# Rank weights on 128 partitions, a block-diagonal wkr, one copy of qrT, and new orders, in a gated cross-attention block with an FFN

## The chip, the cores and the metric

One core of a Trainium2 chip runs the whole kernel. The metric is the device time of one execution in microseconds; the median of several runs is quoted. The profile is of one execution.

## The reference

```
x = x + tanh(g_xattn) * attention(layernorm(x), ctx_512)      # x (4, 256, 256), ctx (4, 256, 64)
x = x + tanh(g_ffn)   * ffn(layernorm(x))

attention, 16 heads, K = 128, DCQ = 192, R = 64, D_C = 64:
  q_hk   = hidden_q @ Wq.T                 # per head 128
  q_big  = q_hk @ w_kc_q                   # 128 -> 192
  q_r    = q_big @ W_qr                    # 192 -> 64
  k_r    = rope(kv_c) @ W_kr               # 64 -> 64
  attn   = softmax(q_r @ k_r.T)            # no scale
  out    = ((attn @ rope(kv_c)) @ w_kc_kv) @ Wo.T

ffn: layer_norm; thought = last row @ agg_w + agg_b;
  4 times: thought += gelu(layer_norm(thought) @ d1_w + d1_b) @ d2_w + d2_b
  out = layer_norm(x + sigmoid(x @ gate_w + gate_b) * (thought @ bc_w + bc_b))
```

All is float32.

## The kernel before

The weights on the way from x to the scores are folded first: for each head W_qr and w_kc_q make qrT (64 x 128), qrT and W_kr make qk (128 x 64), and qk with Wq makes a part of A (foldA), so that the scores of a head are (x_norm A) kv^T. In the same way w_kc_kv and Wo make B (foldB). Heads go in four groups of four (NG = 4, HG = 4). Where precision needs it, a float32 operand is split: ScalarE writes a rounded half (A_hi, xT_hi, q_split), VectorE the rest by subtraction (A_lo, xT_lo), and TensorE adds three products (split_product, lines 898 to 902).

x goes in eight units of 128 rows (NU = 8): units 0 to 3 mix rows of all four batches, the last rows of each batch first, units 4 to 7 take one batch each. Steps of a unit or pair of units: x_stats (mean and variance on VectorE; POOL makes rstd, lines 550 to 558), x_norm, xT (transposes), gq (q of a group for two units), smax (scores for the row maxima, VectorE reduces them, line 749), shiftT (the maxima as a row), q_hi_load (a DMA that moves half of q to the other partitions), st (transposed scores, ScalarE's Exp makes probs), pv, ctxT, out and out_rest, y_stats, y_norm, yT, gate, and at the end f_y, f_pre, f_norm and the store. The FFN's thought chain (c_stats, thoughtT, agg, up, down, downT, bc, bc_rows) runs beside it from unit 0's last rows; its weights are cut into three bfloat16 parts by POOL (w_parts, lines 559 to 573: 8 chunks of d1_w, then 8 of d2_w, which is loaded into the same tile w_rest once the first eight are done, lines 483 to 485).

The order of the work on every engine is written out by hand-held tables: SLOTS gives each step a slot on each engine that takes part, make_plan sorts them, and each engine goes through its list in order, waiting on semaphores. SP issues the loads, all in one queue. PSUM is four rings of two banks: qk and smax; qrT and st; foldB and pv; all others. A step on TensorE waits until its bank is free (claim).

The steps that are changed: load_wqr and load_wkcqT, two DMAs for each group, on 96 partitions (the 192 of DCQ as 96 x 2), load_wkrT on 64 partitions; qrT on TensorE (lines 928 to 939), 8 products per group with 96 rows; the two halves of its result in PSUM, for odd and even heads, are copied to the same 64 partitions of qrT, the odd one by ScalarE (line 607), then the even one by VectorE (line 725), which waits for ScalarE; qk (lines 940 to 952), 8 products per group with 64 rows and 64 columns. WARM is five products on cleared data at the start (line 906), keep five at the end (line 1067).

Of the kernel before, what the change touches and what calls it, by code (L numbers as in the profile page):

```python
# [33 lines left out]
HG = 4  # L34
NG = H // HG
JQ = DCQ // 2
# [31 lines left out]
        "ctxT": (61, 67, 107, 108, 127, 137, 170, 178, 204, 214, 238, 239, 258, 264, 268, 270),  # L68
        "out": (77, 121, 143, 187, 234, 245, 267, 271),
        "out_rest": (79, 122, 145, 188, 235, 246, 269, 272),  # L70
        "yT": (116, 153, 198, 231, 251, 257, 273, 275),
        "gate": (132, 161, 230, 243, 254, 262, 274, 277),
        "thoughtT": (98, 111, 135, 158, 190, 211),
        "agg": (101,),
        "up": (117, 138, 173, 194),
        "down": (123, 146, 181, 201),
        "downT": (126, 149, 186, 205),
        "bc": (216,),
        "bc_rows": (221, 224, 228),
# [2 lines left out]
    "dve": {
        "kvT": (0, 7),
        "qrT": (3, 5, 8, 9),
        "foldA": (11, 14, 22, 24),
        "foldB": (32, 35, 45, 46),
        "x_stats": (1, 2, 12, 13, 15, 16, 21, 23),
        "x_norm": (4, 6, 17, 18, 39, 52, 70, 71),
        "xT": (10, 31, 69, 130),
        "gq": (19, 20, 28, 30, 38, 44, 51, 55, 79, 81, 88, 89, 141, 148, 150, 171),  # L90
        "smax": (25, 26, 27, 29, 33, 34, 36, 37, 40, 41, 42, 43, 47, 48, 49, 50, 57, 58, 60, 61, 63, 64, 66, 67, 68,
# [14 lines left out]
        "down": (110, 131, 157, 172),
        "downT": (113, 135, 159, 176),
# [1 line left out]
        "f_y": (80, 127, 204, 205, 222, 224, 240, 244),
        "f_pre": (195, 196, 212, 213, 225, 228, 242, 245),  # L110
        "f_norm": (202, 203, 217, 218, 235, 236, 246, 247),
    },
    "act": {
        "g_tanh": (30,),
        "kvT": (0, 3),
        "qrT": (1, 2, 7, 8),
        "qk": (4, 5, 11, 14),
        "foldA": (9, 10, 15, 16),
        "foldB": (20, 21, 24, 25),
        "xT": (6, 19, 46, 74),  # L120
        "gq": (12, 13, 17, 18, 22, 26, 32, 33, 47, 49, 53, 54, 81, 85, 86, 100),
        "shiftT": (23, 36, 51, 59, 71, 92, 109, 126),
# [1090 lines left out]
```

## Time and profile before

| | |
|---|---|
| time, median of 3 runs | 212.63 us (212.58 to 213.01) |
| the profiled execution | 213.38 us |
| its span, first to last instruction | 211.4 us |
| busy in the span | TensorE 193.6, VectorE 169.2, ScalarE 96.6, POOL 71.9 us |
| mean granted TensorE clock | 0.949 |

The span leaves out 2.0 us of the execution that lie around the instructions. PE is TensorE, DVE VectorE, ACT ScalarE, SPq the queue of SyncE that issues the DMAs. A matmul instruction's duration includes the filling of the array, so the durations of single ones overlap; a merged row gives the time from the first start to the last end. One float32 product is two instructions in these rows. Times are in us from the start of the span.

### The profile page before, as it was taken

The page shows a single profiled execution, that of the slowest core. Times are in us where ns is not written, and L with a number is a line of the kernel's source. Part 1 is how long each engine was busy: PE and PEld are TensorE (multiplying, and loading weights), DVE is VectorE, ACT ScalarE, POOL GpSimd, SP SyncE. Part 2 cuts the span into 40 slices and gives each one's busy share as a digit, 9 for nine tenths or more (in the row PEclk, how much of TensorE's full clock was granted, in tenths as well). Part 3 has the DMA queues.
Part 4 walks back from the last instruction along what each step waited for, and adds up shares of the span by engine and source line. Part 5 has one row for each costly group of instructions (what it writes and reads, how often), then busy time and mean ns, then how long its engine had stood idle before and what let it go on. Part 6 is the DMA issues. An engine that isn't in the chain of part 4 may idle for free.

```text
span 211.4 us, 6214 instructions
## 1 busy us (share of the span) xinstructions
PE 193.6 (92%) x2533; PEld 169.7 (80%) x2533; DVE 169.2 (80%) x399; ACT 96.6 (46%) x177; POOL 71.9 (34%) x151
## 2 busy tenths in 40 slices
PE   7289979999999999999999999999999999998860
PEld 5078969679889997889999998999887888887730
DVE  4742699999799999996995999395973787899975
ACT  2215354443954355555193567548325243471120
...
GB/s 172 229 250 337 416 416 238 102 5 99 3 199 105 0 5 102 51 3 3 33 72 3 28 75 5 3 0 3 5 172 31 2 3 51 0 44 13 25 25 50
DMA packets 10499, 17.85 MB, mean 84 GB/s; under 512 B 1052, under 2 KB 6436, under 8 KB 9960
## 3 DMA queue, kind: packets, MB, share of 16 engines
...
## 4 chain that ended last, share of the span: by engine, by line
PE 57%; DVE 20%; POOL 8%; DMA 5%; issue 5%; ACT 2%; SPq 1%; POOLq 0%; DVEq 0%; ACTq 0%
PE ps L1032 9%; PE ps L1019 7%; PE ps L1000 6%; PE ps L1021 6%; PE ps L900 4%; DMA wqr<-in_wqr 4%; PE ps L901 4%; PE ps L902 4%; PE ps L936 4%; DVE row_max L749 3%; DVE bn L675 2%; PE ps L1121 2%; PE ps L1110 2%; PE ps L1081 2%; PE ps L1042 2%
## 5 line engine op out<-in xcount | busy, mean ns | idle before, releaser
L638 ACT ACTIVATE probs<-ps 128x512 f32<-128x512 f32 x64 | 36.2, 596 | 33.8 <-PE ps L1021 32.9
L749 DVE TENSOR_REDUCE row_max<-ps 128x2 f32<-128x512 f32 x64 | 41.7, 681 | 5.6 <-PE ps L1000 5.1
L556 POOL TENSOR_SCALAR var_eps<-mean_var 128x1 f32<-128x1 f32 (+1 forms) x29 | 7.3, 251 | 114.0 <-DVE mean_var L676 113.4
L1032 PEld LDWEIGHTS ps<-kv,probs 128*64 128x64 f32 x1024 | 31.2, 137 | 3.0 <-issue 2.0
L1032 PE MATMUL ps<-kv,probs 128*64 128x65 f32 x1024 | 33.6, 223 | 0.0
L1019 PE MATMUL ps<-q_hi,kv_lo 128*128 128x512 f32 x64 | 28.3, 443 | 0.2 <-DMA q_hi<-shift 0.2
L1021 PE MATMUL ps<-q_split,kv_hi 128*128 128x512 f32 x64 | 25.5, 398 | 0.0
L1000 PE MATMUL ps<-kv_hi,q_split 128*128 128x256 f32 x128 | 24.9, 300 | 0.4 <-DVE q_split L743 0.4
L1000 PEld LDWEIGHTS ps<-kv_hi,q_split 128*128 128x128 f32 x128 | 19.1, 189 | 3.9 <-issue 1.9
L900 PE MATMUL ps<-xT_lo,A_hi 128*128 128x256 f32 x64 | 18.9, 295 | 0.1
L900 PE MATMUL ps<-B_lo,ctxT_hi 128*128 128x256 f32 x64 | 18.5, 289 | 0.0
L901 PE MATMUL ps<-xT_hi,A_hi 128*128 128x256 f32 x64 | 18.1, 282 | 0.0
L902 PE MATMUL ps<-xT_hi,A_lo 128*128 128x256 f32 x64 | 18.0, 282 | 0.0
L901 PE MATMUL ps<-B_hi,ctxT_hi 128*128 128x256 f32 x64 | 18.0, 282 | 0.0
L902 PE MATMUL ps<-B_hi,ctxT_lo 128*128 128x256 f32 x64 | 18.0, 282 | 0.0
L557 POOL TENSOR_TENSOR rstd<-var_eps,minus_half 128x1 f32<-128x1 f32 (+1 forms) x29 | 17.1, 590 | 2.4
L624 ACT ACTIVATE q_split<-ps 64x512 fp32r<-64x512 f32 x16 | 9.4, 590 | 16.7 <-PE ps L902 16.7
L641 ACT ACTIVATE ctxT_hi<-ps 128x512 fp32r<-128x512 f32 x16 | 9.4, 597 | 13.2 <-PE ps L1042 13.2
L762 DVE TENSOR_TENSOR ctxn<-ps,prob_sum_inv 128x256 f32<-128x256 f32 x32 | 13.6, 424 | 1.1
L1019 PEld LDWEIGHTS ps<-q_hi,kv_lo 128*128 128x128 f32 x64 | 12.3, 193 | 2.3 <-issue 0.7
L1021 PEld LDWEIGHTS ps<-q_split,kv_hi 128*128 128x128 f32 x64 | 12.4, 194 | 1.0
L900 PEld LDWEIGHTS ps<-xT_lo,A_hi 128*128 128x128 f32 x64 | 12.1, 190 | 0.9 <-DVE q_split L743 0.3
(133 smaller groups left out, 405.7 us busy)
## 6 DMA issues: line engine op xcount, KB each, us to landing
...
wq<-in_wq SPq DMA_DIRECT2D x4, 512.0 KB, 12.5
...
w_rest<-in_d_w SPq DMA_DIRECT2D x2, 1024.0 KB, 12.8
...
wqr<-in_wqr SPq DMA_DIRECT2D x4, 192.0 KB, 10.1
x<-in_x SPq DMA_DIRECT2D x2, 256.0 KB, 10.3
```

The costliest lines, as they stand in the source:

```text
L557: pool.tensor_tensor(rstd[0:rows, n:n + 1], var_eps[0:rows, n:n + 1], minus_half[0:rows, :], ALU.pow).then_inc(rstd_made, 1)
L624: act.activation(q_part(U, j, 0, lower), q_from(e, lower), ACT.Copy)
L638: act.activation(probs[:, n % PROBS_BUFS, lb, :], bank(e), ACT.Exp).then_inc(free[place[e]], 1)
L749: dve.reduce_max(row_max[:, s % 2, 2 * j:2 * j + 2], bank(e).rearrange("p (h l) -> p h l", h=2), AX.X).then_inc(free[place[e]], 1)
L762: dve.tensor_tensor(dst, r[:, :, 0:DC], prob_sum_inv[:, :].unsqueeze(2).to_broadcast([P, HG, DC]), ALU.mult).then_inc(free[place[e]], 1)
L900: pe.matmul(dst, a_hi, b_lo, start=first, stop=False)
L901: pe.matmul(dst, a_hi, b_hi, start=False, stop=False)
L902: return pe.matmul(dst, a_lo, b_hi, start=False, stop=last)
L1000: ins = pe.matmul(bank(e)[:, i * S:(i + 1) * S], q_split[s // 2 % 2][:, c:c + P], kv_hi2[:, kv_batch(s, j // 2), :], start=True, stop=True)
L1019: pe.matmul(bank(e), kv_lo[:, b, ls], q_hi[:, u % 2, g * HG * P:(g + 1) * HG * P], start=True, stop=False)
L1021: pe.matmul(bank(e), kv_hi2[:, b, ls], q_split[U % 2][:, q], start=False, stop=True).then_inc(done, 1)
L1032: ins = pe.matmul(bank(e)[q:q + 64, hh * (DC + 1):(hh + 1) * (DC + 1)], probs[:, n % PROBS_BUFS, lb, hh * P + q:hh * P + q + 64], kv1[:, k ...
```

## The change

The rank weights of a pair of heads are laid out in one tensor of 128 partitions and 640 columns: the first 128 of the 192 rows of w_kc_q (transposed) for the even head, then, for both heads, the last 64 rows, the even head's on partitions 0 to 63 and the odd head's on 64 to 127, then the first 128 of the odd head, then the four pieces of W_qr to match, with zeros where the other head's rows stand. One DMA loads the two pairs of a group (load_rank, 640 KB). qrT is again 8 products per group, now over 128 rows. Its result keeps odd heads on the upper 64 partitions, and ScalarE alone copies it, 128 x 256. wkr is block-diagonal over a pair of heads (128 x 128, 512 KB in all), so qk is 4 products per group over 128 rows and 128 columns.

All orders are new. On TensorE qrT 0 goes ahead of kvT 0, foldA 0 and 1 ahead of qk 2, qrT 3 behind gq 0,1, and keep behind the last gate. On VectorE x_stats 0 and 1 come first, and x_stats 2 to 6 ahead of gq 0,0. On POOL out 0 (it scales two rows by the tanh) goes ahead of x_stats 3, and all 16 w_parts ahead of y_stats 0. On SP the order is consts, ctx, rank 0, rank 1, x 0, wkr, rank 2, wq 0, wq 1, x 1, the rest of x, rows, rank 3, wq 2, wq 3, w1, wkckv, wo 0, wo 1, q_hi 0, gate and agg, q_hi 1, shiftT 0, w2, shiftT 1; before it was ctx, consts, wkcqT 0, wkrT, wkcqT 1, wqr 0, x 0, wqr 1, wkcqT 2 and 3, wqr 2 and 3, wq 0, wq 1, x 1, the rest of x, wq 2, wq 3, wkckv, wo 0, w1, wo 1, gate and agg, rows, q_hi 0, vecs, shiftT 0, q_hi 1, shiftT 1, w2.

```diff
-JQ = DCQ // 2
+RANK = 3 * P + 4 * R
...
-        "kvT": (0, 3),
-        "qrT": (1, 2, 7, 8),
+        "kvT": (1, 3),
+        "qrT": (0, 2, 7, 13),
-        "foldA": (9, 11, 15, 16),
+        "foldA": (8, 9, 15, 16),
...
-        "keep": (276,),
+        "keep": (277,),
...
-        "kvT": (0, 7),
-        "qrT": (3, 5, 8, 9),
-        "foldA": (11, 14, 22, 24),
...
+        "kvT": (2, 5),
+        "foldA": (7, 9, 19, 22),
+        "x_stats": (0, 1, 8, 10, 11, 12, 13, 18),
+        "x_norm": (3, 4, 16, 17, 36, 37, 57, 60),
+        "y_norm": (78, 111, 136, 165, 190, 210, 231, 235),
...
-        "x_stats": (1, 2, 3, 4, 5, 6, 7, 8),
-        "out": (24, 24, 24, 24, 24, 24, 24, 24),
-        "y_stats": (20, 30, 31, 36, 39, 40, 47, 50),
-        "w_parts": (9, 10, 11, 12, 13, 14, 15, 16, 17, 18, 19, 21, 22, 25, 26, 27),
-        "c_stats": (23, 28, 29, 34, 35),
-        "f_y": (32, 33, 41, 43, 48, 49, 51, 52),
-        "f_pre": (37, 38, 42, 44, 45, 46, 53, 54),
+        "x_stats": (1, 2, 3, 5, 6, 7, 8, 9),
+        "out": (4, 4, 4, 4, 4, 4, 4, 4),
+        "y_stats": (26, 30, 33, 36, 37, 44, 49, 50),
+        "w_parts": (10, 11, 12, 13, 14, 15, 16, 17, 18, 19, 20, 21, 22, 23, 24, 25),
...
-        "load_wkcqT": (2, 4, 8, 9),
-        "load_wqr": (5, 7, 10, 11),
-        "load_wkrT": (3,),
...
-        "load_w1": (20,),
-        "load_w2": (29,),
...
+        "load_rank": (2, 3, 6, 12),
+        "load_wkr": (5,),
...
+        "load_w1": (15,),
...
+        "load_w2": (23,),
...
-        wkrT = sb("wkrT", [R, H * DC], F32, stage)
-        wqr = sb("wqr", [JQ, H, 2, R], F32, stage)
-        wkcqT = sb("wkcqT", [JQ, H, 2, P], F32, stage)
-        qrT = sb("qrT", [R, 2, HG * P], F32, stage)
+        wkr = sb("wkr", [P, H // 2, 2 * DC], F32, stage)
+        rank = sb("rank", [P, H // 2, RANK], F32, stage)
+        qrT = sb("qrT", [P, 2, HG // 2 * P], F32, stage)
...
+                if name == "load_rank":
+                    ps2 = slice(HG // 2 * e[1], HG // 2 * (e[1] + 1))
+                    sp.dma_start(rank[:, ps2, :], t["rank"][:, ps2, :]).then_inc(rank_in[e[1]], 16)
...
-                    act.activation(qrT_cols(e[1], 1), bank(e)[upper, 0:HG // 2 * P].rearrange("p (i k) -> p i k", k=P),
-                                   ACT.Copy).then_inc(qrT_odd_copied, 1)
+                    act.activation(qrT[:, e[1] % 2, :], bank(e)[:, 0:HG // 2 * P], ACT.Copy
+                                   ).then_inc(free[place[e]], 1)
...
-                if name == "qrT":
-                    dve.wait_ge(qrT_odd_copied, e[1] + 1)
-                    filled(dve, e)
-                    dve.tensor_copy(qrT_cols(e[1], 0), bank(e)[lower, 0:HG // 2 * P].rearrange("p (i k) -> p i k", k=P)
-                                    ).then_inc(free[place[e]], 1)
...
-                    pe.wait_ge(wqr_in[g], 16)
-                    pe.wait_ge(wkcqT_in[g], 16)
-                    for hh in range(0, HG, 2):
-                        for j in range(2):
+                    pe.wait_ge(rank_in[g], 16)
+                    for i in range(HG // 2):
+                        w = rank[:, HG // 2 * g + i, :]
+                        for part in range(2):
                             for odd in range(2):
-                                ins = pe.matmul(bank(e)[64 * odd:64 * odd + 64, hh // 2 * P:(hh // 2 + 1) * P],
-                                                wqr[:, HG * g + hh + odd, j, :], wkcqT[:, HG * g + hh + odd, j, :],
-                                                start=(j == 0), stop=(j == 1))
+                                keys = w[:, P:2 * P] if part else w[:, 2 * P * odd:2 * P * odd + P]
+                                queries = w[:, 3 * P + R * (2 * part + odd):3 * P + R * (2 * part + odd + 1)]
+                                ins = pe.matmul(bank(e)[64 * odd:64 * odd + 64, i * P:(i + 1) * P], queries, keys,
+                                                start=(part == 0), stop=(part == 1))
                     ins.then_inc(done, 1)
                 if name == "qk":
 
                     g = e[1]
                     taken(pe, ("qrT", g))
                     if g == 0:
-                        pe.wait_ge(wkrT_in, 16)
-                    for hh in range(HG):
-                        h = HG * g + hh
+                        pe.wait_ge(wkr_in, 16)
+                    for i in range(HG // 2):
                         for k in (0, 64):
-                            ins = pe.matmul(bank(e)[k:k + 64, hh * DC:(hh + 1) * DC],
-                                            qrT[:, g % 2, hh * P + k:hh * P + k + 64],
-                                            wkrT[:, h * DC:(h + 1) * DC], start=True, stop=True)
+                            ins = pe.matmul(bank(e)[k:k + 64, 2 * i * DC:2 * (i + 1) * DC],
+                                            qrT[:, g % 2, i * P + k:i * P + k + 64],
+                                            wkr[:, HG // 2 * g + i, :], start=True, stop=True)
...
+    keys = a["L0_xattn_w_kc_q"].transpose(0, 2, 1)
+    queries = a["L0_xattn_W_qr"]
+    rank = np.zeros((H // 2, P, RANK), np.float32)
+    wkr = np.zeros((P, H // 2, 2 * DC), np.float32)
+    for odd in range(2):
+        rows = slice(64 * odd, 64 * odd + 64)
+        wkr[rows, :, DC * odd:DC * (odd + 1)] = a["L0_xattn_W_kr"][odd::2].transpose(2, 0, 1)
+        rank[:, :, 2 * P * odd:2 * P * odd + P] = keys[odd::2, 0:P]
+        rank[:, rows, P:2 * P] = keys[odd::2, P:DCQ]
+        rank[:, :, 3 * P + R * odd:3 * P + R * (odd + 1)] = queries[odd::2, 0:P]
+        rank[:, rows, 3 * P + R * (2 + odd):3 * P + R * (3 + odd)] = queries[odd::2, P:DCQ]
```

## Rows read from the trace of the kernel before

**Rows 1.** Windows, four stretches: us, busy us (instructions) of each engine, clock, DMA

```profile
core 0: us, PE busy (x) PEld busy (x) DVE busy (x) ACT busy (x) POOL busy (x), PEclk, DMA share, GB/s
4.00:18.00 14.00, 9.27 (x78) 7.21 (x78) 8.21 (x12) 3.50 (x7) 6.03 (x12) 0.68 1.02 240
18.00:34.00 16.00, 14.78 (x230) 13.59 (x231) 10.71 (x26) 7.15 (x14) 4.21 (x12) 0.85 1.02 409
23.40:45.60 22.20, 20.48 (x255) 16.82 (x249) 21.07 (x42) 10.60 (x20) 14.69 (x32) 1.00 0.64 238
45.60:200.50 154.90, 152.36 (x2124) 136.12 (x2124) 130.21 (x325) 78.35 (x143) 45.07 (x89) 0.99 0.16 39
```

**Rows 2.** Chain of waits, in order of time: start us, us, what

```profile
3.34 7.86 DMA wqr<-in_wqr
```

**Rows 3.** Timeline of SP's queue: start us, us, issue

```profile
1.17 0.42 SPq L444 DMA_DIRECT2D consts<-in_consts  x1
...
12.64 0.43 SPq L477 DMA_DIRECT2D w_rest<-in_d_w  x1
```

**Rows 4.** DMA issues of 1.1 to 1.6 us: size, us to landing

```profile
consts<-in_consts SPq DMA_DIRECT2D x1, 192.0 KB, 2.7
```

**Rows 5.** The two loads of w_rest, at 12.64 and 58.4 us

```profile
DMA to landing us min/median/max: 6.3/12.8/19.4
```

**Rows 6.** Windows at two changes of the TensorE clock

```profile
9.00:9.25 0.25, 0.00 (x0) 0.00 (x0) 0.23 (x1) 0.00 (x0) 0.00 (x0) 0.51 0.94 205
22.50:23.00 0.50, 0.50 (x18) 0.50 (x16) 0.00 (x0) 0.30 (x1) 0.00 (x0) 0.84 1.09 418
```

**Rows 7.** Timeline of PE: start us, us, instructions

```profile
11.25 3.80 PE L936 MATMUL ps<-wkcqT,wqr 96*64 96x128 f32 x32 [4.18 <-DMA wqr<-in_wqr]
...
16.02 1.97 PE L949 MATMUL ps<-wkrT,qrT 64*64 64x64 f32 x32
...
24.18 1.15 PE L962 MATMUL ps<-qk,wq 128*64 128x64 f32 x32
...
28.52 0.68 PE L949 MATMUL ps<-wkrT,qrT 64*64 64x64 f32 x16
...
37.85 0.66 PE L925 MATMUL ps<-consts,xn 128*128 128x128 f32 x4
```

**Rows 8.** Groups by shape, first 50 us: busy us, mean ns, idle before

```profile
L675 DVE BATCH_NORM_STATS2 bn<-x 128x6 f32<-128x256 f32 x8 | 3.4, 424 | 2.9 <-DMA x<-in_x 2.8
...
L725 DVE COPY qrT<-ps 64x256 f32<-64x256 f32 x4 | 1.7, 413 | 5.5 <-ACT qrT L607 5.5
L611 ACT ACTIVATE qk<-ps 128x256 f32<-128x256 f32 x4 | 1.5, 382 | 0.4 <-PE ps L949 0.3
L607 ACT ACTIVATE qrT<-ps 64x256 f32<-64x256 f32 x4 | 1.5, 380 | 9.1 <-PE ps L936 9.1
L676 DVE BATCH_NORM_AGGREGATE mean_var<-bn 128x2 f32<-128x6 f32 x8 | 1.5, 182 | 0.3
```

**Rows 9.** Timeline of DVE

```profile
5.51 3.47 DVE L698 MEMSET q_hi<- 64x4096 f32 x1 [0.80 <-issue]
...
24.32 0.69 DVE L730 TENSOR_TENSOR A_lo<-ps,A_hi 128x512 fp32r<-128x512 f32 x1 [0.20 <-ACT A_hi L615]
...
44.86 0.69 DVE L743 TENSOR_TENSOR q_split<-ps,q_split 64x512 fp32r<-64x512 f32 x1
...
73.03 0.40 DVE L682 TENSOR_SCALAR y<-x,mean_var,rstd 128x256 f32<-128x256 f32 x1
```

**Rows 10.** Timeline of POOL

```profile
34.37 0.41 POOL L569 CAST d_parts<-w_rest 128x256 bf16<-128x256 f32 x1
...
52.30 0.67 POOL L572 TENSOR_TENSOR d_parts<-w_rest,d_parts 128x256 bf16<-128x256 f32 x1
64.74 0.40 POOL L569 CAST d_parts<-w_rest 128x256 bf16<-128x256 f32 x1 [11.77 <-DMA w_rest<-in_d_w]
...
72.29 0.57 POOL L557 TENSOR_TENSOR rstd<-var_eps,minus_half 128x1 f32<-128x1 f32 x1
```

More of the change, by code:

```diff
@@ L62 @@
-        "shiftT": (35, 55, 90, 104, 131, 176, 210, 242),
[5 rows of a table removed]
[L68 to L79, printed above, removed]
-        "keep": (276,),
+        "foldA": (8, 9, 15, 16),
+        "foldB": (23, 25, 32, 35),
+        "xT": (6, 24, 44, 139),
+        "gq": (11, 12, 19, 22, 28, 31, 37, 41, 86, 89, 96, 97, 160, 161, 170, 195),
+        "smax": (17, 18, 20, 21, 26, 27, 29, 30, 33, 36, 38, 42, 43, 47, 48, 52, 54, 57, 59, 62, 63, 67, 70, 71, 75,
+            77, 80, 82, 83, 85, 87, 88, 94, 95, 98, 99, 107, 112, 114, 120, 121, 124, 126, 130, 136, 148, 152, 153, 165,
+            166, 171, 173, 179, 187, 202, 204, 208, 214, 215, 219, 222, 224, 226, 229),
@@ new lines @@
+        "shiftT": (34, 56, 76, 105, 127, 169, 209, 240),
[5 rows of a table added]
+        "ctxT": (66, 72, 115, 116, 142, 149, 180, 181, 205, 213, 233, 236, 261, 262, 268, 270),
+        "out": (81, 122, 154, 190, 221, 242, 267, 271),
+        "out_rest": (84, 123, 155, 191, 223, 244, 269, 272),
+        "yT": (108, 132, 201, 232, 248, 252, 273, 275),
+        "gate": (131, 175, 207, 247, 251, 258, 274, 276),
+        "thoughtT": (103, 119, 145, 164, 193, 216),
+        "agg": (110,),
+        "up": (128, 151, 178, 196),
@@ L81 @@
+        "down": (135, 156, 186, 203),
+        "downT": (138, 159, 189, 212),
+        "bc": (220,),
+        "bc_rows": (225, 227, 228),
+        "keep": (277,),
     },
     "dve": {
-        "kvT": (0, 7),
-        "qrT": (3, 5, 8, 9),
-        "foldA": (11, 14, 22, 24),
[L86 to L90, printed above, removed]
@@ L106 @@
[L106 to L107 removed]
+        "up": (112, 130, 151, 167),
+        "down": (116, 133, 156, 170),
+        "downT": (119, 137, 157, 178),
         "bc": (185,),
[L109 to L111 removed]
+        "f_y": (79, 114, 199, 202, 207, 219, 237, 240),
+        "f_pre": (194, 195, 200, 211, 216, 223, 238, 241),
@@ L112 @@
+        "f_norm": (196, 201, 206, 213, 218, 226, 242, 243),
     },
     "act": {
[L114 to L122, printed above, removed]
[3 rows of a table removed]
-        "ctxT": (40, 43, 61, 62, 70, 72, 89, 93, 108, 110, 123, 125, 135, 143, 144, 145),
@@ L127 @@
-        "yT": (63, 79, 103, 119, 132, 136, 146, 147),
-        "gate": (82, 105, 130, 131, 137, 142, 148, 149),
-        "up": (66, 73, 91, 101),
-        "bc_rows": (115, 116, 118),
+        "g_tanh": (11,),
+        "kvT": (1, 3),
+        "qrT": (0, 2, 7, 14),
+        "qk": (4, 5, 10, 15),
+        "foldA": (8, 9, 16, 17),
+        "foldB": (21, 22, 26, 27),
+        "xT": (6, 20, 31, 74),
+        "gq": (12, 13, 18, 19, 23, 24, 28, 34, 51, 52, 55, 56, 85, 86, 90, 103),
+        "shiftT": (25, 37, 48, 59, 67, 88, 109, 125),
[3 rows of a table added]
@@ L131 @@
+        "ctxT": (42, 45, 65, 66, 77, 80, 95, 96, 107, 113, 120, 123, 141, 143, 144, 145),
+        "yT": (61, 69, 105, 119, 130, 134, 146, 147),
+        "gate": (72, 94, 111, 131, 135, 139, 148, 149),
+        "up": (68, 81, 97, 104),
+        "bc_rows": (114, 115, 116),
     },
@@ L193, in steps @@
     return {
-        "load_consts": [()], "load_wkcqT": [(g,) for g in groups], "load_wqr": [(g,) for g in groups],
-        "load_wkrT": [()], "load_wq": [(g,) for g in groups], "load_x": [(U,) for U in halves], "load_x_rest": [()],
+        "load_consts": [()], "load_rank": [(g,) for g in groups],
+        "load_wkr": [()], "load_wq": [(g,) for g in groups], "load_x": [(U,) for U in halves], "load_x_rest": [()],
         "load_ctx": [()], "load_wo": [(i,) for i in halves], "load_wkckv": [()], "load_rows": [()], "load_w1": [()], "load_w2": [()], "load_bc_w": [()],
@@ L428, in ctx_from @@
             return bank(e).rearrange("p (b g q) -> p b g q", b=2, g=H // 2)
-        def qrT_cols(g, odd):
-            return qrT[:, g % 2, :].rearrange("p (i two k) -> p i two k", two=2, k=P)[:, :, odd, :]
         lower, upper = slice(0, 64), slice(64, 128)
@@ L1179, in laid_out @@
         "ctx": a["ctx_512"].reshape(NB, LB, P, DC).transpose(2, 0, 1, 3),
-        "wkrT": a["L0_xattn_W_kr"].transpose(2, 0, 1).reshape(R, H * DC),
-        "wqr": a["L0_xattn_W_qr"].reshape(H, JQ, 2, R).transpose(1, 0, 2, 3),
-        "wkcqT": a["L0_xattn_w_kc_q"].reshape(H, K, JQ, 2).transpose(2, 0, 3, 1),
+        "wkr": wkr,
+        "rank": rank.transpose(1, 0, 2),
         "wq": a["L0_xattn_Wq"].reshape(H, K, D).transpose(1, 0, 2),
```

82 lines of the change are left out of this document (36 added, 46 removed), and 24 rows, old and new, of the table SLOTS.

## The prediction

> **What bounds the kernel now.** I read the windows by stage first, then the chain of waits, then the timelines of SP, PE, DVE and POOL, and the groups by shape. The windows show three regimes. From 45.6 us to 200.5 us TensorE is busy 152.4 of 154.9 us [rows 1], so whatever brings that stage forward brings the end forward, unless something else becomes late. From 23.4 to 45.6 us VectorE is busy 21.1 of 22.2 us [rows 1]: it subtracts rounded halves, takes row maxima and x's statistics, and TensorE waits for it. Before that both wait for loads: the chain starts with the DMA of wqr, 7.86 us from its issue [rows 2], and TensorE, idle for 4.18 us, begins qrT 0 at 11.25 [rows 7].
>
> The loads explain why. With the 16 DMA engines busy all the time (share 1.02), 240 GB/s move from 4 to 18 us and 409 GB/s from 18 to 34 [rows 1]. The break is where the last rank load is through; those of before stand on 96 or 64 partitions, those after on 128. Beside it the clock: TensorE falls to 1.2 GHz (granted 0.51) at 9.0 us, in its idle stretch, and is back at 2.4 GHz only within 22.5 to 23.0 [rows 6], having worked without a break from 11.25.
>
> **The loads after.** 192 + 256 KB of consts and ctx end at 1.17 + 2.7 = 3.9 us [rows 3, 4], and still do: the two change places. Four rank loads of 640 KB and wkr of 512 KB follow instead of 2304 + 256 KB, that is 512 KB more, and four issues fewer. All rows are now 128 partitions by 4 to 5 KB (the nearest: wq, w_rest, in the 409 GB/s stretch), so I take 409 GB/s. 640 KB then take 1.60 us, 512 KB 1.28. Landings: rank 0 at 5.5, rank 1 at 7.1, x 0 at 7.7, wkr at 9.0, rank 2 at 10.6, wq 0 at 11.9, wq 1 at 13.2, x 1 at 13.8, the rest of x at 15.1, the rows at 16.1, rank 3 at 17.7, wq 2 at 19.0, wq 3 at 20.2, w1 at 22.8 (before: 12.64 + 19.4 = 32.0 [rows 3, 5]). The other bound is that 240 GB/s last to 18 us whatever the layout; then wq 0 lands at 3.9 + 3.28 MB / 240 GB/s = 17.6.
>
> The Trainium skill (SBUF — State Buffer, "Door 1: The DMA port swizzle") has a mechanism for the slow stretch: partitions 0 to 63 sit behind eight of the sixteen ports, so 96 partitions load the crowded ports as 128 would. By its 435 GB/s, the early rank loads, x 0 and wkrT (30 KB per partition) would take an estimated 9.0 us; the trace gives them some 14, so the ports alone don't account for it. A figure of the skill speaks against the change's rate: DMA: Bandwidth & Descriptors, "Specifications", limits one core's HBM share to about 358 GB/s. By that w1 would land at 25.5 (estimate), 2.7 us later; the trace disagrees, 409 GB/s over 16 us [rows 1].
>
> **The front of TensorE and VectorE.** qrT passes the same columns as before, with 128 rows instead of 96: 3.80 us for two groups at 1.2 GHz [rows 7], 1.9 a group, and an estimated 0.95 at 2.4 GHz. qk passes the same columns in half as many instructions; a group takes 0.68 us at full clock [rows 7], I take no gain (bounds 0 and half of it, 0.34), since VectorE hides it. The copy of qrT by ScalarE covers 128x256 instead of 64x256: 382 against 380 ns [rows 8], so nothing; ScalarE is idle before it. VectorE loses four copies, 1.7 us, which stood in a stretch where it waited 5.5 us for them [rows 8]; that too is worth nothing by itself, and the 0.41 us it takes from each hand-over is covered by kvT and xT.
>
> At full clock TensorE ends WARM at 5.9, then qrT 0, kvT 0, qrT 1, kvT 1 (0.95 and about 0.6 each) at 9.0, as wkr lands, and qk 0 and 1 at 10.4. VectorE's clearing of q_hi ends at 9.0 [rows 9]. Behind it: two x_stats (0.61 plus a gap, 0.67 each [rows 8]) to 10.3, kvT 0 to 11.0, two x_norm to 11.9. xT's transposes take 0.66 [rows 7], to 12.5; qrT 2 to 13.5; foldA 0 takes 1.15 [rows 7], to 14.6; ScalarE's half 0.6; so VectorE begins A_lo 0 at 15.3 instead of 24.32 [rows 9]. From there to the end of gq 1,0 (45.55 [rows 9]) VectorE's list holds the same operations in another order, and every load they need (wq 3 at 20.2) is in before its turn. So the stretch keeps its 21.2 us, and the front moves by 9.0.
>
> **What takes part of it back.** y_norm 0 waits for a rstd from POOL. In the new order all sixteen w_parts stand ahead of it; before, only eleven did. POOL begins them at the later of w1 (22.8) and x_stats 7, for which VectorE has from 15.3: eight-fold work of A_lo, x_stats, gq and x_norm, 0.69 x 2 + 6 x 0.67 + 2 x 1.4 + 2 x 0.43 = 9.1 us, plus 0.8 of POOL: 25.2. From there eight chunks 18.6 us (34.37 to 52.97), the load of w2 6.3 from its issue (it now stands ahead of shiftT 1 on SP, and goes out at once; before, POOL waited 11.77 us), eight more chunks 18.5, and rstd 0.9 [rows 5, 10]: 44.4 in all, so 69.6. VectorE's new list has three maxima and gq 2,0 more ahead of y_norm 0, five reads of 128x512 at 0.69 [rows 9], 3.4 us: it would be wanted at 73.0 + 3.4 - 9.0 = 67.4. VectorE stands 2.2 us, in order, and the smax banks behind it fill, so TensorE stands too. Net 9.0 - 2.2 = 6.8 us.
>
> Other moves. out 0 on POOL, ahead of x_stats 3, waits for the rows (16.1) and tanh, and takes some 2 us; x_norm 3 needs the result at about 24, so gq 0,0 and 0,1 on VectorE cover it. SP stands at load_w2 until about 43.8; behind it is shiftT 1, wanted at about 50. q_hi 0 follows wo 1, which by the same rate is in at 29.2, about when gq 0,3 ends. keep goes behind the last gate: five products of 512 columns, by foldA's row (2048 in 1.15 us) an estimated 1.4 us no longer in front of it; VectorE is still at unit 6 then, so I take 0 and keep 0 to 1.1 as a gain. The rest of the new order has the same work in a stage where TensorE is full; I take 0 and allow 0.5 either way.
>
> **The sum.** The profiled execution took 213.38 us (span 211.4 and 2.0 around it), 0.75 above the median of the runs. 213.38 - 6.8 = 206.6 on its own scale, 212.63 - 6.8 = 205.8 for the median. A change under 0.2% (0.4 us) could not be told from none.
>
> **Rivals.** (a) The clock falls anyway. TensorE now has work in most of 6 to 10.4 us, where before it had little between WARM and 11.25, but it still waits there for loads and for VectorE; and at half clock it ran from 11.25 to past 22.5 us before it got the full clock back [rows 6, 7]. Worked out: 5.9, two qrT 3.8, two kvT 2.1, two qk 2.0, xT 1.3, qrT 2 1.9, foldA 0 2.3, ScalarE 0.6: A_lo 0 at 19.9, 4.6 us worse. Gain 2.2, time 210.4. The skill (TensorE: Matmul & The Clock Gate, "Part 1") agrees that low recent activity brings the low level.
> (b) The layout does not do what it says: 240 GB/s belong to the start of the kernel, not to 96 partitions. Then wq 0 at 17.6, A_lo 0 at 19.3, gain 2.8, time 209.8. For it: no 128-partition load ran by itself before 18 us, so nothing shows 409 GB/s that early. Against: the break lies where the layout changes.
> (c) TensorE works through y_norm's stall from its queue (gq 2,1, st, pv stand behind): gain 9.0, with keep and the orders up to 10, time 203.6 down to 202.5.
> (d) Slower: y_norm 0 stuck behind POOL. If the slow rate lasts through w1 (7.75 MB at 240 GB/s), w1 lands at 36.2, y_norm 0 comes at 80.6 instead of 73.0 + 3.4 = 76.4: 4.2 slower, 216.8. It decides from a w1 later than 32.0. Against it: 409 GB/s in the stretch of the very same loads.
> (e) Nothing is left because a later wait (the chain of the thoughts, whose agg, up and down now stand later in TensorE's list) holds the end: 212.6.
>
> **Numbers.** Forecast 0.52, (a) 0.20, (b) 0.09, (c) 0.11, (d) 0.04, (e) 0.04. Range 202.5 to 210.5: from (c) to (a) and (b). Faster 0.92, same 0.03, slower 0.05 (part of (e) falls on either side).
>
> **What would show it.** qrT 0 beginning near 6 us; above 350 GB/s from 4 us on; granted clock 1.00 through 9 to 15 us; A_lo 0 near 15; POOL's first chunk near 25 instead of 34.4; y_norm 0 near 69.6 with VectorE waiting for POOL. Wrong would be made by half clock past 12 us, by loads that land a third later, or by a wait behind 80 us that the trace of before does not have.

## The result and the profile after

The changed kernel takes 205.62 us (median of 4 runs, 204.75 to 206.37) against 212.61 us (4 runs, 212.18 to 213.01) beside it: ratio 0.967, 95% interval 0.9625 to 0.9716. The forecast was 205.8 us in a range of 202.5 to 210.5. The profiled execution took 205.26 us, with a span of 203.4. Here and below, ratios and intervals compare undisturbed runs alone, while a median also takes in runs that the chip slowed by some per cent, so a ratio can be nearer to 1 than that of the two medians.

First the windows by stage, which answer to [rows 1]; columns as there.

```profile
core 0: us, PE busy (x) PEld busy (x) DVE busy (x) ACT busy (x) POOL busy (x), PEclk, DMA share, GB/s
4.00:9.00 5.00, 3.07 (x22) 1.98 (x21) 4.19 (x2) 0.00 (x0) 4.46 (x8) 1.00 0.93 277
9.00:18.00 9.00, 8.61 (x134) 7.18 (x132) 4.42 (x10) 5.61 (x12) 1.67 (x4) 0.81 1.03 404
4.00:18.00 14.00, 11.67 (x153) 9.16 (x152) 8.61 (x12) 5.61 (x12) 6.13 (x12) 0.88 0.99 358
9.00:9.50 0.50, 0.50 (x6) 0.47 (x4) 0.00 (x0) 0.38 (x1) 0.00 (x0) 0.71 1.05 311
12.50:13.00 0.50, 0.50 (x8) 0.29 (x8) 0.50 (x2) 0.18 (x1) 0.42 (x3) 0.88 0.99 410
```

The stretch that moved 240 GB/s before moves 358 now, but not evenly: 277 GB/s to 9 us, 404 after it. TensorE's clock falls at 9 us as before, to 1.2 GHz, and is back within 12.5 to 13.0; before it stayed low until past 22.5 [rows 6].

The chain of waits starts with another load than before [rows 2] (first and later pieces: start us, us, what):

```profile
2.58 8.36 DMA x<-in_x
...
10.96 0.44 DVE bn L663
...
12.93 0.69 POOL rstd L545
...
14.20 0.63 PE ps L908 x4
14.83 1.02 PE ps L921 x16
15.86 0.95 PE ps L945 x32
...
16.83 0.61 ACT A_hi L603
```

It is now x 0, landing at 10.94 us, then its statistics, its transposes, qrT 2 and foldA 0 that lead to A_lo 0. TensorE's timeline (start us, us, instructions) shows that the first rank products (7.93 and 9.80) are done before x's transposes are wanted and are no longer the link:

```profile
7.93 1.09 PE L921 MATMUL ps<-rank 128*64 128x128 f32 x16 [1.93 <-DMA rank<-in_rank]
...
9.80 1.97 PE L921 MATMUL ps<-rank 128*64 128x128 f32 x16
...
12.71 1.09 PE L932 MATMUL ps<-wkr,qrT 128*64 128x128 f32 x16
14.20 0.63 PE L908 MATMUL ps<-consts,xn 128*128 128x128 f32 x4 [0.39 <-DVE xn L670]
```

VectorE and POOL, for [rows 9] and [rows 10]:

```profile
10.96 0.43 DVE L663 BATCH_NORM_STATS2 bn<-x 128x6 f32<-128x256 f32 x1 [1.97 <-DMA x<-in_x]
17.46 0.69 DVE L713 TENSOR_TENSOR A_lo<-ps,A_hi 128x512 fp32r<-128x512 f32 x1 [1.27 <-ACT A_hi L603]
...
38.20 0.69 DVE L726 TENSOR_TENSOR q_split<-ps,q_split 64x512 fp32r<-64x512 f32 x1
...
70.52 0.41 DVE L670 TENSOR_SCALAR y<-x,mean_var,rstd 128x256 f32<-128x256 f32 x1
```

```profile
27.02 0.40 POOL L557 CAST d_parts<-w_rest 128x256 bf16<-128x256 f32 x1
...
50.48 0.40 POOL L557 CAST d_parts<-w_rest 128x256 bf16<-128x256 f32 x1 [4.85 <-DMA w_rest<-in_d_w]
...
69.41 0.57 POOL L545 TENSOR_TENSOR rstd<-var_eps,minus_half 128x1 f32<-128x1 f32 x1
```

A_lo 0 starts at 17.46 us instead of 24.32: 6.9 earlier. The end of gq 1,0 comes at 38.89 instead of 45.55: 6.7 earlier, so VectorE's stretch kept its length (21.4 us). y_norm 0 starts at 70.52 with no wait in front of it; POOL's rstd is done at 69.98. y_norm 0 stands 2.5 us before its old place with 3.4 us more work ahead of it, 5.9 in all. From y_norm 0 to the end, 132.9 us against 138.4: 5.5 less, of which 3.4 is the work that now lies ahead; the other 2.1 us is taken up below.

### The profile page after: what moved, and what is told of

It reads as the page before. It is cut to its first block, busy times and chain, and to the rows that moved or that the text cites. A ratio compares the mean times of both kernels' runs of the same rounds, so it can differ in the third digit from the quotient of the medians.

```text
span 203.4 us, 6138 instructions
## 1 busy us (share of the span) xinstructions
PE 188.3 (93%) x2501; PEld 164.3 (81%) x2501; DVE 167.3 (82%) x395; ACT 96.2 (47%) x177; POOL 73.4 (36%) x151
## 4 chain that ended last, share of the span: by engine, by line
PE 62%; DVE 22%; DMA 6%; issue 5%; POOL 2%; ACT 1%; SPq 1%; POOLq 0%; DVEq 0%
PE ps L1015 11%; PE ps L983 7%; PE ps L883 7%; PE ps L885 6%; PE ps L884 6%; PE ps L1002 5%; PE ps L1004 4%; DMA x<-in_x 4%; DVE row_max L732 4%; DVE bn L663 3%; PE ps L1104 2%; PE ps L1025 2%; PE ps L1093 2%; PE ps L1064 2%; DVE fin_in L862 2%
## 5 line engine op out<-in xcount | busy, mean ns | idle before, releaser
L1002 PE MATMUL ps<-q_hi,kv_lo 128*128 128x512 f32 x64 | 27.7, 432 | 0.3 <-DMA q_hi<-shift 0.3
L983 PE MATMUL ps<-kv_hi,q_split 128*128 128x256 f32 x128 | 25.5, 300 | 0.3 <-DVE row_max L732 0.2
L1004 PE MATMUL ps<-q_split,kv_hi 128*128 128x512 f32 x64 | 25.2, 394 | 0.0
L545 POOL TENSOR_TENSOR rstd<-var_eps,minus_half 128x1 f32<-128x1 f32 (+1 forms) x29 | 18.1, 624 | 2.4
L883 PEld LDWEIGHTS ps<-xT_lo,A_hi 128*128 128x128 f32 x64 | 12.2, 190 | 1.3 <-DVE A_lo L713 0.8
```

What stands on the lines that cost most here:

```text
L545: pool.tensor_tensor(rstd[0:rows, n:n + 1], var_eps[0:rows, n:n + 1], minus_half[0:rows, :], ALU.pow).then_inc(rstd_made, 1)
L883: pe.matmul(dst, a_hi, b_lo, start=first, stop=False)
L983: ins = pe.matmul(bank(e)[:, i * S:(i + 1) * S], q_split[s // 2 % 2][:, c:c + P], kv_hi2[:, kv_batch(s, j // 2), :], start=True, stop=True)
L1002: pe.matmul(bank(e), kv_lo[:, b, ls], q_hi[:, u % 2, g * HG * P:(g + 1) * HG * P], start=True, stop=False)
L1004: pe.matmul(bank(e), kv_hi2[:, b, ls], q_split[U % 2][:, q], start=False, stop=True).then_inc(done, 1)
```

## The experiments

The twelve kernels ran in three groups on chips that did not repeat alike: the kernel before gave medians of 213.31 (212.02 to 217.15), 212.79 (208.18 to 216.89) and 212.25 us (208.75 to 216.67) beside them. So ratios are compared within a group, and places in the traces carry the finer readings. Those too vary by themselves: in its three profiles the changed kernel starts A_lo 0 at 17.46, 16.86 (after_again) and 17.89 us (after_third).

**layout_only: the new layout under the old orders.** The changed kernel with all the orders of before.

```diff
-        "load_rank": (2, 3, 6, 12),
-        "load_wkr": (5,),
+        "load_rank": (2, 4, 8, 10),
+        "load_wkr": (3,),
...
-        "kvT": (1, 3),
-        "qrT": (0, 2, 7, 13),
+        "kvT": (0, 3),
+        "qrT": (1, 2, 7, 8),
```

> The changed layout (rank weights on 128 partitions, wkr block-diagonal, one copy by ScalarE) with the orders of the kernel before. Theory 1, the loads are the lever and the layout brings their rate: the last rank load is through near 14 us instead of 18, VectorE begins A_lo 0 near 19.5 to 20.5 instead of 24.3, the kernel takes 207.5 to 209. Theory 2, the orders bring the gain: 211.5 to 212.6. The stage behind 45 us is unchanged in order, so a gain in the front that is lost behind it would show as A_lo 0 early and a time near 212.

**orders_only: the new orders with the old layout.** The three rank loads take the places of rank and wkr; both halves of qrT's copy are back.

```diff
-        "load_wkcqT": (2, 4, 8, 9),
-        "load_wqr": (5, 7, 10, 11),
-        "load_wkrT": (3,),
+        "load_wkcqT": (2, 3, 6, 12),
+        "load_wqr": (2.5, 3.5, 6.5, 12.5),
+        "load_wkrT": (5,),
```

> The layout of the kernel before (96 and 64 partitions, two loads for each group, two copies of qrT) with the new orders. Theory 1: the loads still run at about 240 GB/s until the rank weights of three groups are in; wq 0 now stands behind three groups instead of four, 576 KB less, so A_lo 0 comes some 2.5 us earlier than 24.3 and the kernel takes 209 to 210.5. Theory 2: 206 to 207.

**padded: only the partitions changed.** The kernel before, its rank weights and wkr filled up with zeros to 128 partitions: 1 MB more to load, the products still read 96 and 64 of them.

```diff
-        wqr = sb("wqr", [JQ, H, 2, R], F32, stage)
-        wkcqT = sb("wkcqT", [JQ, H, 2, P], F32, stage)
+        wqr = sb("wqr", [P, H, 2, R], F32, stage)
+        wkcqT = sb("wkcqT", [P, H, 2, P], F32, stage)
...
-        "wqr": a["L0_xattn_W_qr"].reshape(H, JQ, 2, R).transpose(1, 0, 2, 3),
+        "wqr": padded(a["L0_xattn_W_qr"].reshape(H, JQ, 2, R).transpose(1, 0, 2, 3)),
```

> The kernel before with wkcqT, wqr and wkrT padded with zeros to 128 partitions; a third more bytes for the first two and twice for the last, the products read the same 96 and 64 partitions, all orders as before. If the rate of a load hangs on how many partitions it covers: from 9 us on above 390 GB/s, the last rank load through near 15 us instead of 18.2 although 1 MB more is moved, and 210 to 211.5. If the low rate belongs to the number of bytes or to the first 18 us of the kernel: the rate stays near 240, the last rank load comes at 20 us or later, and the kernel takes 214 or more.

Windows of the three kernels in that order (two of layout_only, three of orders_only, two of padded):

```profile
4.00:9.00 5.00, 2.70 (x17) 1.94 (x18) 4.19 (x2) 1.18 (x2) 4.46 (x8) 0.88 0.94 332
9.00:18.00 9.00, 7.43 (x78) 5.99 (x76) 3.96 (x9) 3.45 (x8) 1.58 (x4) 0.69 1.00 375
```

```profile
9.00:18.00 9.00, 6.66 (x85) 5.78 (x86) 4.55 (x11) 4.48 (x9) 1.61 (x4) 0.76 1.03 297
18.00:29.00 11.00, 8.23 (x128) 7.75 (x126) 8.68 (x21) 4.43 (x10) 5.76 (x12) 0.81 1.03 359
29.00:34.00 5.00, 5.00 (x77) 4.76 (x74) 1.34 (x4) 1.58 (x3) 4.01 (x9) 0.50 0.91 372
```

```profile
4.00:9.00 5.00, 2.69 (x9) 1.48 (x8) 4.19 (x2) 1.18 (x2) 4.45 (x8) 1.00 0.89 300
9.00:18.00 9.00, 5.20 (x40) 4.14 (x42) 3.37 (x9) 0.92 (x3) 1.59 (x4) 0.55 1.02 375
```

layout_only: 208.08 us, ratio 0.9788 (0.9739 to 0.9837), A_lo 0 at 20.19 us. orders_only: 211.20, ratio 0.9948 (0.9905 to 0.9991), A_lo 0 at 19.97. padded: 214.48, ratio 1.0061 (1.0025 to 1.0097), A_lo 0 at 25.61. Three readings:

The rate follows the partitions that the loads cover. padded moves 300 and then 375 GB/s, 348 over the 14 us in which the kernel before moved 240 [rows 1]; the number of loads and the length of a row on a partition are as before, so neither of these was the brake. It is slower all the same, where 210 to 211.5 us were expected: more bytes go first (x 0 is in at 13.92 us instead of 12.49), and the clock is low for most of the stretch from 9 us (0.55), so a rate is not yet an early landing. The layout of the change gets the rate without the padding.

By ratio and 212.6 us, the layout alone gives 4.5 us and the orders alone some 1.1. The changed kernel did not run in this group: it gave 7.0 in its own, and clear_by_act below, which differs from it only in who clears q_hi, gave 5.9 here. So the layout is two thirds to three quarters of the gain, and 0.3 to 1.4 us would be what the two give only together; the intervals, about 1 us to either side each, don't settle that.

The orders alone bring A_lo 0 forward by 4.35 us, more than the 2.5 expected, and lose it again. TensorE, working without a break from 29 to 34 us, does so at 1.2 GHz, and VectorE is busy for 1.3 of these 5 us. Ahead of it stands this wait (PE timeline):

```profile
28.27 1.12 PE L949 MATMUL ps<-wkrT,qrT 64*64 64x64 f32 x16 [2.77 <-DVE qrT L725]
```

VectorE's half of the copy of qrT 3 stands behind the first two gq in its list, and TensorE waits for it. This asks what the copy by ScalarE alone is worth:

**split_copy: the changed kernel with two half copies again.**

```diff
-                    act.activation(qrT[:, e[1] % 2, :], bank(e)[:, 0:HG // 2 * P], ACT.Copy
-                                   ).then_inc(free[place[e]], 1)
+                    act.activation(qrT[upper, e[1] % 2, :], bank(e)[upper, 0:HG // 2 * P], ACT.Copy
+                                   ).then_inc(qrT_odd_copied, 1)
...
+                if name == "qrT":
+                    dve.wait_ge(qrT_odd_copied, e[1] + 1)
+                    filled(dve, e)
+                    dve.tensor_copy(qrT[lower, e[1] % 2, :], bank(e)[lower, 0:HG // 2 * P]).then_inc(free[place[e]], 1)
```

> The changed kernel with qrT copied out in two halves as before, the upper 64 partitions by ScalarE, then the lower 64 by VectorE (first in its list, between kvT 0 and x_norm 0, behind xT 0, behind gq 0,1). Theory: each copy costs VectorE 0.41 us; the two of the first groups stand ahead of x_stats and x_norm, where VectorE waits for x 0 anyway, the last stands in the full stretch. 0.3 to 0.8 us slower than the changed kernel. If the copy by ScalarE alone is worth nothing: within 0.2 us.

207.82 us, ratio 0.9819 (0.9767 to 0.9872); the changed kernel beside it (after_again) 206.64, ratio 0.9791 (0.9737 to 0.9845). The intervals overlap, so the times don't show a loss; the traces do. A_lo 2 waits, and y_norm 0 comes at 73.07 us instead of 69.48. Of these 3.6 us, 1.0 is a front that was later already (A_lo 0 at 17.90 against 16.86), within what the changed kernel does by itself; 2.5 arise behind it, not the 0.3 to 0.8 expected. PE, then DVE timeline of split_copy:

```profile
25.81 1.12 PE L938 MATMUL ps<-wkr,qrT 128*64 128x128 f32 x8 [3.00 <-DVE qrT L715]
```

```profile
29.30 0.69 DVE L719 TENSOR_TENSOR A_lo<-ps,A_hi 128x512 fp32r<-128x512 f32 x1 [2.32 <-ACT A_hi L605]
```

The copy costs VectorE 0.42 us, and TensorE 3.0 us of waiting, by its place behind four subtractions and no longer by its length. The place (after the first two gq) was mine; a better one may cost less, and was not tried.

**clear_by_act: does the clearing of q_hi slow the loads?** VectorE's memset of 64x4096 replaced by four ScalarE instructions that write zeros.

```diff
-            dve.memset(q_hi[64:P, :, :].bitcast(F32), 0.0).then_inc(q_hi_cleared, 1)
...
+            for i in range(4):
+                ins = act.activation(q_hi[64:P, i // 2, S * NB * (i % 2):S * NB * (i % 2 + 1)],
+                                     kv_lo[64:P, :, :].rearrange("p b l -> p (b l)").bitcast(F32), ACT.Copy, scale=0.0)
```

> The changed kernel, but the 3.5 us clearing of q_hi is done by ScalarE (four copies scaled by zero, from about 4.7 to 9 us) instead of VectorE. In the changed kernel the loads run at 277 GB/s from 4 to 9 us and at 412 from then on, and VectorE's clearing ends at 9.0. If that clearing slows the loads: the rate from 5.5 to 9 us rises to about 400, rank 0 and x 0 land 1 to 2 us earlier, and the kernel takes 204 to 205. If the low rate belongs to the start of the kernel: the rate is 270 to 290 from 4 to 9 us again, x 0 lands at 11.0 again, and the time is that of the changed kernel within 0.5 us (VectorE waits for x 0 anyway; ScalarE is ready for qrT 0 only just in time).

206.28 us, ratio 0.9723 (0.964 to 0.9806): as the changed kernel. 286 GB/s from 4 to 9 us, A_lo 0 at 17.86 us. So it does not matter which engine clears. ScalarE's clearing falls in the same 5 us, and a kernel without any was not tried; but padded and front_loads move 379 and 425 GB/s from 8 to 9 us while VectorE clears, so the clearing need not slow a load.

**after_again** is the changed kernel once more, beside split_copy and the next two.

> The changed kernel once more, as the measure for the three kernels beside it. Expected as before: about 0.967 of the kernel before.

206.64 us, ratio 0.9791 (0.9737 to 0.9845), 4.4 us by ratio where the first group had 7.0, and the intervals don't meet: the gain is some 2 to 3 per cent, and its size differs between chips. y_norm 0 at 69.48 us, here with a wait of 0.24 for POOL: its rstd and VectorE arrive together.

**y_early: y_stats 0 on POOL behind the eleventh chunk, as before.**

```diff
-        "y_stats": (26, 30, 33, 36, 37, 44, 49, 50),
+        "y_stats": (20.5, 30, 33, 36, 37, 44, 49, 50),
```

> The changed kernel with y_stats 0 on POOL behind the eleventh w_parts chunk, as in the kernel before, instead of behind the sixteenth. In the trace of the changed kernel POOL has the rstd of y_stats 0 at 69.98 us and VectorE, busy until 70.5, begins y_norm 0 at 70.52, so it does not wait. Theory 1 (no price of w_parts at this front): the time stays within 0.4 us of the changed kernel's, up (w_parts 1 ends 0.9 us later for down 0) or down. Rival (the forecast's 2.2 us stall is there, only hidden in the profile): 1 us or more faster.

213.08 us, ratio 1.0142 (1.009 to 1.0194): 6.4 us slower than after_again, the whole gain gone. Neither theory said so. POOL's and then VectorE's timeline:

```profile
69.88 0.22 POOL L544 TENSOR_SCALAR var_eps<-mean_var 128x1 f32<-128x1 f32 x1 [10.47 <-DVE mean_var L664]
...
83.45 0.56 POOL L545 TENSOR_TENSOR rstd<-var_eps,minus_half 4x1 f32<-4x1 f32 x1
```

```profile
84.05 0.40 DVE L670 TENSOR_SCALAR thought_norm<-last_rows,mean_var,rstd 4x256 f32<-4x256 f32 x1 [5.94 <-POOL rstd L545]
```

With w2 in early, POOL reaches y_stats 0 at 59.4 us, ten before VectorE has its input; it stands, in order, and the last five chunks and the rstd of the thoughts behind them come late, the latter at 83.45 us where after_third has it at 75.76. (1.5 of these 7.7 us is a later front, A_lo 0 at 19.36 against 17.89; the other 6.2 agree with the 6.4 of the medians.) TensorE, busy 3.05 of the 5 us from 78 to 83, falls to 1.2 GHz behind it. So all chunks ahead of y_stats 0, which the forecast booked as a cost, is what the early w2 wants.

**w1_late: w1 loaded behind wo 1.**

```diff
-        "load_w1": (15,),
+        "load_w1": (18.5,),
```

> The changed kernel with the load of w1 behind wo 1 in SP's queue, so that it lands near 31 us instead of 25.9 and POOL begins w_parts 4 us later. If the in-order wait of VectorE at y_norm 0 passes on one for one: y_norm 0 comes near 74, 3.5 us later than 70.5, and the kernel takes 3 to 3.5 us more than the changed one. If TensorE works through the wait from its queue and VectorE catches up: at most 1 us more.

212.52 us, ratio 1.0022 (0.9979 to 1.0064): 5.9 us slower than after_again. VectorE's timeline:

```profile
75.87 0.41 DVE L670 TENSOR_SCALAR y<-x,mean_var,rstd 128x256 f32<-128x256 f32 x1 [4.71 <-POOL rstd L545]
```

w1 lands at 32.7 us, later than the 31 expected. Against the first profile of the change, whose front ends at the same time (A_lo 0 at 17.46 and 17.47), POOL's rstd is 5.9 us late, y_norm 0 5.4, of which VectorE stands 4.71, and the span is 6.1 longer (209.5 against 203.4). The stall at y_norm 0 passes on in full: TensorE has no queue that hides it, which is against rival (c), and rival (d)'s mechanism is real, only its condition did not hold. The expected 3 to 3.5 us had left out that POOL was just in time already.

The last four ran together: **after_third**, the changed kernel; **warm8**, with more warming; **front_loads** and **front_and_pool**, an attempt at a faster front.

> The changed kernel once more, on the chip of the three runs beside it. Both theories: 205 to 207 us, ratio near 0.968 to 0.98 as before.

```diff
-WARM = 5
+WARM = 8
```

> The changed kernel with 8 instead of 5 matmuls that warm TensorE at the start. Theory: the front is a chain through loads and VectorE (the x 0 load lands at 10.96 us, A_lo 0 at 17.46), so a clock that stays up between 9 and 12 us can shorten only qrT 1 and the two qk, which end before xT 0 is wanted; A_lo 0 stays within 0.3 us of 17.46, the time within 0.5 us of the control. Rival (the half clock from 9.2 to 12.6 us is on the path): A_lo 0 comes 1 us or more earlier and the time falls by about 1 us.

after_third 206.08 us, ratio 0.9781 (0.9649 to 0.9914); warm8 205.70, ratio 0.979 (0.9671 to 0.9909). after_third's PE and DVE timelines, then warm8's:

```profile
10.54 1.98 PE L921 MATMUL ps<-rank 128*64 128x128 f32 x16
```

```profile
17.89 0.69 DVE L713 TENSOR_TENSOR A_lo<-ps,A_hi 128x512 fp32r<-128x512 f32 x1 [1.21 <-ACT A_hi L603]
```

```profile
9.57 1.09 PE L921 MATMUL ps<-rank 128*64 128x128 f32 x16
10.60 0.65 PE L900 MATMUL ps<-consts,kv 128*65 128x128 f32 x4
12.67 1.09 PE L932 MATMUL ps<-wkr,qrT 128*64 128x128 f32 x16 [1.42 <-DMA wkr<-in_wkr]
14.54 0.63 PE L908 MATMUL ps<-consts,xn 128*128 128x128 f32 x4 [0.77 <-DVE xn L670]
```

```profile
17.80 0.69 DVE L713 TENSOR_TENSOR A_lo<-ps,A_hi 128x512 fp32r<-128x512 f32 x1 [1.27 <-ACT A_hi L603]
```

In one, qrT 0 and qrT 1 take twice as long as in the other; A_lo 0 starts 0.09 us apart, far less than the changed kernel varies by itself. What warm8 saves, TensorE waits for wkr (1.42 us) and for x's norm (0.77). The clock does not set the front now; the loads do.

**front_loads: x 0 and wkr ahead of rank 1, wq 0 and 1 ahead of rank 2**, and foldA 0 and 1 ahead of qrT 2.

```diff
-        "load_rank": (2, 3, 6, 12),
-        "load_wkr": (5,),
-        "load_wq": (7, 8, 13, 14),
-        "load_x": (4, 9),
+        "load_rank": (2, 5, 8, 12),
+        "load_wkr": (4,),
+        "load_wq": (6, 7, 13, 14),
+        "load_x": (3, 9),
...
-        "foldA": (8, 9, 15, 16),
+        "foldA": (6.3, 6.6, 15, 16),
```

> The changed kernel with x 0 and wkr loaded ahead of rank 1, wq 0 and wq 1 ahead of rank 2, and foldA 0 and 1 ahead of qrT 2 on TensorE and ScalarE. Theory (the late load of x 0 is what the front lost against the forecast): x 0 lands at about 9 us instead of 10.96, A_lo 0 starts at 15 to 16 us instead of 17.46. VectorE then reaches y_norm 0 about 1.5 us earlier, but POOL's chain (first chunk at 27.02, rstd of y_stats 0 at 69.4) moves by less than that, since its first chunk waits for w1, which lands at 25.9; so the net is a gain of 0.3 to 1 us and VectorE waits about 1 us for POOL before y_norm 0. Rival (the loads at the start are slow whatever comes first): whichever load is second or third is slow, x 0 stays near 10.5 us and A_lo 0 near 17; time as the control.

**front_and_pool: front_loads, and w1 ahead of wq 2, the last x_stats ahead of x_norm 2.**

```diff
-        "x_stats": (0, 1, 8, 10, 11, 12, 13, 18),
+        "x_stats": (0, 1, 8, 10, 11, 12, 13, 15.5),
...
-        "load_w1": (15,),
+        "load_w1": (12.5,),
```

> The kernel front_loads with w1 loaded ahead of wq 2 and the last x_stats ahead of the third x_norm on VectorE, so that POOL may begin its chunks near 25 us instead of 27. Theory (the front and POOL's chain are both at the edge, so both must move for a gain): first chunk at 24.5 to 25.5 us, rstd of y_stats 0 at 67 to 68.5, no wait at y_norm 0, 1.2 to 2 us faster than the control. Rival: wq 2 and wq 3 come late by w1's 2.5 us, foldA 2 waits for them and TensorE or VectorE loses what the rest gained: time as the control or slower.

208.71 us, ratio 0.9899 (0.9739 to 1.006), and 207.43 us, ratio 0.9885 (0.9748 to 1.0023): neither is faster than after_third beside them (2.6 and 1.4 us slower by the medians), and the intervals don't tell them from it. front_loads, DVE and then PE:

```profile
9.02 0.43 DVE L663 BATCH_NORM_STATS2 bn<-x 128x6 f32<-128x256 f32 x1
...
17.05 0.69 DVE L713 TENSOR_TENSOR A_lo<-ps,A_hi 128x512 fp32r<-128x512 f32 x1 [0.70 <-ACT A_hi L603]
```

```profile
11.54 1.09 PE L921 MATMUL ps<-rank 128*64 128x128 f32 x16 [1.60 <-DMA rank<-in_rank]
```

x 0 is in before VectorE asks for it, 1.9 us earlier than in the change, and A_lo 0 gains 0.4 us (0.8 against after_third), no more than the changed kernel varies: now rank 1 is late, 11.5 us. The first group needs consts, ctx, rank 0 and 1, x 0, wkr and wq 0 in any order, and the last of them decides; the expectation had put the loss on one load. What A_lo 0 won is lost behind it (y_norm 0 at 71.50 us, after_third 71.35); that this is qk 2, which comes later (19.00 us against 17.55) with the first gq behind it, is argued and not shown. In front_and_pool POOL's first chunk comes at 28.15 us, later than in the control (27.44), not at 25: its x_stats wait for A_lo 0 (18.15) and that for rank 1 (12.65), so w1 was not its limit. The forecast of this run fell. No tried version beats the change.

## Why the prediction was right

For the profiled execution the forecast was 206.6 us from 213.38, and 205.26 came; for the medians 205.8, and 205.62 came. The mechanism was right: loads bound the front, and the layout speeds them up. The number is nearer than its terms. The front and the stall behind it were each off by some 2 us, in opposite directions and for one reason, as shown below; that two errors in POOL's chain cancelled as well was luck. By its own steps:

**What bounds the front: right.** Loads set it. padded shows that 240 GB/s were the 96 and 64 partitions, not the start of the kernel, so rival (b) fails as the whole story. In padded the loads take little longer than before (qrT 0 starts at 11.58 us against 11.25 [rows 7], x 0 is in 1.4 later) and move a third more bytes, for wkr twice as many; the rate over 4 to 18 us is 348 against 240 GB/s, 1.45 times. By the Trainium skill's port rule (SBUF — State Buffer, "Door 1: The DMA port swizzle") the crowded ports carry the same with 96 and with 128 partitions; the trace agrees roughly as to the time, and the rule would give a factor of 1.33 (an estimate for the loads of 96 alone). The Trainium skill's limit of about 358 GB/s (DMA: Bandwidth & Descriptors, "Specifications"), a stack's bandwidth halved between two cores, is again passed by this one core: 404 GB/s from 9 to 18 us.

**Landings at 409 GB/s from 3.9 us: the mis-sized term.** The page's DMA issues, and the landings of the two w_rest, for [rows 4] and [rows 5]:

```profile
wkr<-in_wkr SPq DMA_DIRECT2D x1, 512.0 KB, 9.1
```

```profile
DMA to landing us min/median/max: 4.8/10.4/16.1
```

rank 0 was forecast at 5.5 and let TensorE go at 7.93; x 0 at 7.7, landed at 10.94; wkr (issued at 3.05) at 12.2 against 9.0; w1 (issued at 9.82) at 25.9 against 22.8. All are about 3 us late from x 0 on, and w1 comes 13.7 us behind wkr as forecast (13.8): the rate was right from 9 us and wrong before. At 277 instead of 409 GB/s the five microseconds from 4 to 9 move 0.66 MB less, 1.6 us at the later rate. So (b) held in part for these 5 us. Most of the rest is that loads don't land in their turn. Windows from 3.9 us to the landing of x 0 and of w1, then, in the kernel before, to the end of VectorE's wait for x 0:

```profile
3.90:10.94 7.04, 5.11 (x38) 3.69 (x38) 4.29 (x2) 1.41 (x3) 4.46 (x8) 0.88 0.95 300
3.90:25.92 22.02, 18.72 (x266) 15.54 (x265) 16.13 (x30) 10.19 (x21) 11.90 (x24) 0.92 1.00 377
```

```profile
3.90:12.49 8.59, 3.86 (x22) 2.82 (x22) 4.97 (x4) 1.18 (x2) 4.46 (x8) 0.80 1.00 235
```

When x 0 lands, 2.11 MB have moved, where rank 0, rank 1 and x 0 are 1.57; when w1 lands, 8.30 MB of the 7.75 up to it. Some 0.5 MB of what stands behind had moved by then, an estimated 1.3 us at 409 GB/s (the loading of instructions, 0.39 MB in the whole execution, can be only a part). The sum of landings, bytes ahead divided by the rate, left this out; the trace of before had it too, 2.02 MB moved at x 0 for 1.51 MB up to it.

**A_lo 0 at 15.3: it came at 17.46.** From the first x_stats the chain took 6.5 us against 6.3 forecast (9.0 to 15.3). The miss is the start: x_stats 0 waited until 10.96 for x 0, not only until 9.0 for the memset. The front moved by 6.9 us, not 9.0, and VectorE's stretch behind it kept its length as forecast (21.4 against 21.2).

**A stall of 2.2 us at y_norm 0: it was 0.** POOL's chain ended where it was forecast, by two errors that cancel: first chunk at 27.02 (25.2 forecast), 42.96 from there to the end of rstd (44.4 forecast, w2 being in 4.8 us after its issue and not 6.3), done at 69.98 (69.6). VectorE was forecast for 67.4 by a front 9.0 earlier. With a front of 6.7 its turn is at 69.7, and it came at 70.52. So the two errors are one: what loads took from the front, the stall would have taken a moment later. w1_late shows the edge, 5.9 us for a w1 that comes later, and after_again a wait of 0.24. At y_norm 0 the net was 5.9 us for the forecast 6.8 (6.7 of front, less 0.8 that VectorE lost on the way and that nothing here places), near it for that reason and not because each term held.

**The clock: half right.** It fell (rival (a)'s premise), but for the 3.4 us from some 9.2 to 12.6 instead of 13.7. (a) priced half clock through the whole front at 4.6 us; for what there was of it, after_third and warm8 show a price too small to see (0.09 us), since TensorE waits for wkr and x in the time saved.

**The copy of qrT, worth nothing: true of the old orders, false of the new.** split_copy puts 3 us of TensorE's waiting on it in one place, and 2.5 us at y_norm 0. I took the operation for hidden by the waits of before, and didn't ask who would wait for it in the new lists.

**The rest of the orders at 0.** Behind y_norm 0 the profiled execution gained 2.1 us. Part of it is no doing of the change: in the profiled execution of before the clock fell while TensorE was busy, behind three groups of products of 4 rows (bc_rows); windows and PE timeline of before:

```profile
163.00:164.00 1.00, 1.00 (x4) 0.75 (x3) 0.58 (x1) 0.00 (x0) 0.00 (x0) 0.50 0.08 16
```

```profile
159.49 1.12 PE L1137 MATMUL ps<-bc,consts 4*128 4x256 f32 x4
...
161.66 0.69 PE L1137 MATMUL ps<-bc,row_pick 4*128 4x256 f32 x2
...
162.65 1.91 PE L1081 MATMUL ps<-gate_w,yT 128*128 128x256 f32 x4
```

In the profile after it doesn't fall there; in after_again, with the same code, it does (0.50 from 158 to 160 us). padded gives the price: from y_norm 0 on it runs the very instructions of before, and its clock stays up. Its y_norm 0, then its window there:

```profile
74.35 0.40 DVE L682 TENSOR_SCALAR y<-x,mean_var,rstd 128x256 f32<-128x256 f32 x1
```

```profile
160.00:166.00 6.00, 6.00 (x28) 4.31 (x28) 2.89 (x6) 3.60 (x8) 0.00 (x0) 1.00 0.13 24
```

From there to the end of its span (211.2 us) are 136.9 us against 138.4 in the kernel before, and layout_only, again with the orders of before and a clock that stays up, needs 136.9 too. So 1.5 of the 2.1 us is the fall and 0.6 is left for the orders. Without the fall the profiled executions gain 6.6 us instead of 8.1, near the forecast (6.8) and the medians (7.0).
